# A two-layer attention kernel with new pass timing, one GELU evaluation, scaling on ScalarE, and three PSUM banks for filling units with one for the weighted values

## The chip, the cores and the metric

One core of a Trainium2 chip runs the whole program. The metric is the device time of one execution in microseconds; three executions were timed, and one more was profiled. Engines: TensorE (PE; PEld is its weight loading), VectorE (DVE), ScalarE (ACT), GpSimd (POOL) and SyncE (SP), which only issues DMAs.

## What is computed

Two layers of cross-attention over eight batches of 512 tokens by 512 features, 16 heads of 32. All arithmetic is float32.

```
tgt2 = attention(x Wq', ctx Wk', ctx Wv')[0]       # layer 0: only batch 0 is used
x    = x + tgt2                                    # added to all eight batches
xq, ykv = layer_norm(x, gq, bq), layer_norm(ctx, gkv, bkv)
o    = softmax(q k^T * SCALE) v                    # q = xq Wq, (k, v) = ykv Wkv
x    = x + o Wproj + bproj
h    = gelu(layer_norm(x, gm, bm) W1 + b1)         # exact GELU, 2048 hidden features
x    = x + h W2 + b2
```

## The kernel before

**Precision.** Each float32 operand is split into a high part (rounded to float32r) and a low part (the rest), side by side, and a product is three matmuls (high by high, high by low, low by high). So every evacuation of PSUM is two steps: ScalarE writes the high part, VectorE then subtracts it from the bank and writes the low part. Where a gain and a bias are applied, ScalarE works twice (`affine`), once to the high part and once in place in the bank.

**Passes and ticks.** The attention of layer 0 (batch 0) is pass 0, that of layer 1 for batch n-1 is pass n, 1 to 8. A pass has 16 heads of 4 chunks of 128 keys, 64 ticks. `Plan.core` (L96) puts the three steps of chunk s at three ticks: scores (`ps_s`) at tick t, the transposed, max-shifted weights matmul (`ps_t`) at t + SHIFT, the weighted values (`ps_o`) at t + WEIGH. Between the scores and the weights matmul of a head VectorE takes the row maxima, turns them, and SP sends them by four small DMAs into a row of `q_st` (`load_row`). ScalarE then evaluates the exponential twice, once into the high part `p_hi` and once in place; VectorE makes the low part (POOL for chunk 2 of each head). After the fourth chunk ScalarE moves `ps_o` to `o_raw` (L965, semaphore `o_moved`), and SP's DMAs place it beside the other heads of its group of four (`place_head`); after each group VectorE inverts the sums and POOL joins and scales in four steps (`invert`, `join`).

**Filling units.** All other matmuls are units of 12 matmuls in 4 parts (quarters) of 3, or turns of 4 transposes. Kinds: `a` (turned, normed inputs), `k`, `q`, `v` (projections), `tg` (turned result of pass 0), `out` (projection of the result, Wproj), `ht` (turned, normed h), `hid` (W1), `y2` (W2). `spread` (L81) distributes parts over the three places of each tick: after the scores matmul (0), after the weights matmul (1), after the weighted values (2). Each unit uses one bank of `ps_d`, by its number modulo the number of banks (`bank`, L481), and its first part waits until the unit that had the bank is evacuated. Every pass from 3 on has 16 `hid`, 16 `y2`, 4 `out` and 4 `ht` units of the batch one or two passes back.

**Order.** No engine picks its work: each runs the ticks in order, and within a tick what the tables list, waiting on semaphores. On ScalarE a tick is: evacuations whose unit ended at place 0 or at place 2 of the tick before; a GELU burst; two exponentials; evacuations of units ended at place 1; the `o_raw` move; DMA issues of W1 and W2 pieces (`load_w1`, `load_w2`); the scaling of a norm; weight splits.

**GELU bursts.** Four `hid` units fill one half of `h_st` (128 x 2048). At the burst tick ScalarE evaluates GELU twice over it, into the high part `g_s` (L940) and in place (L941), and POOL subtracts (L1237). Around it ScalarE loads the function table, before the GELU and before the next exponential. The `y2` units placed at the front of the burst tick keep TensorE at work meanwhile. W2 pieces are issued from the tick after the last `y2` unit of the group before, 3 ticks apart.

**Norms.** `norm_ticks` (L249) gives the ticks of statistics (VectorE), inverse deviation (POOL, `inverse_deviation`, L1163) and scaling. The context batches (`y`) and the x batches are scaled by POOL in the staging buffer (`scale_staged`, L1180), the first x batch by VectorE (`scale_x0`), h by ScalarE with `shift` = -mean/deviation as bias (`scale_result`, L918). `X_SUMS` (L324) are POOL's additions of `tgt2` to x.

**The gap.** Between the last weighted values of pass 0 and the first scores of pass 1 are 8 ticks without attention (L128 to L136). There the result of pass 0 is turned (`tg`), added to batch 0 of x, normed, turned (`a10`) and projected (`q1`), stored to DRAM and read back as the first stack (`store`, `load_stack`). A stack is the query and key rows of one head, four DMAs, issued STACK_AHEAD ticks before its scores, once the weights matmuls of the head four before are done. `sync_tables` (L331) gives all ticks of SP's and ScalarE's DMAs.

**Tail.** After pass 8 the last outputs, hidden units and `y2` units run with nothing of a head beside them.

```
                if c == 0:
                    if h >= 2:
                        pe.wait_ge(o_moved, h - 1)
```

These lines (L845 to L847) let TensorE start the weighted values of head h once the head two before has left its bank.

## Time and profile before

| | us |
|---|---|
| median of three timed executions | 2067.64 |
| lowest and highest of them | 2053.57, 2070.22 |
| the profiled execution, its own time | 2060.26 |
| its span, first to last instruction | 2058.3 |

The busy time of an engine is the sum over its instructions, the span is what the metric follows. A matmul's duration overlaps with the next one's, so their pitch is shorter than their mean length. The granted clock is the share of TensorE's full speed that it was given; waits are idle time of an engine with what released it.

### The profile page before, as it was taken

Reading aid. Unit: us, or ns where it says so; the run is one execution under the profiler, and the core shown is the slowest. Engines: PE = TensorE matmul, PEld = TensorE weight load, DVE = VectorE, ACT = ScalarE, POOL = GpSimd, SP = SyncE. Lnnn points to the kernel's source line nnn. Section 1 sums busy time; section 2 is a strip of 40 time slices with the busy share of each in tenths; the row PEclk is TensorE's granted clock in tenths of the full one; section 3 lists DMA queues with packets and bytes.
Section 4 is the critical chain, followed back from the end, with each engine's and each line's share of the span. In section 5 each row is a group of like instructions: output and inputs, shape, how many; then the busy total and the mean of one; then the engine's idle time right before and its main releaser. Section 6 shows DMA issues by size and latency. Waiting matters only on the chain.

```text
span 2058.3 us, 23412 instructions
## 1 busy us (share of the span) xinstructions
PE 1805.1 (88%) x7488; PEld 1365.0 (66%) x7488; DVE 1168.1 (57%) x2008; ACT 1117.8 (54%) x1762; POOL 851.6 (41%) x557
## 2 busy tenths in 40 slices
PE   7899987887887889888899989998988989899898
PEld 5576765665665667666676666676666667677676
DVE  4566654575756556555666565566656656654322
ACT  3455653375656655755665476566556564754211
POOL 0667740477653333434433343433434333433311
PEclk9899998998998899999999999999999999999899
DMA  6689942654643455466366436554663754455243
GB/s 213 227 286 348 381 177 82 204 195 137 209 163 93 141 155 153 134 169 181 114 201 185 146 115 180 165 154 123 195 183 95 205 177 140 137 162 178 94 151 143
DMA packets 156377, 354.65 MB, mean 172 GB/s; under 512 B 28512, under 2 KB 47072, under 8 KB 155360
## 3 DMA queue, kind: packets, MB, share of 16 engines
q1 hardware_dynamic: 119392, 218.92, 34.2%
q10 hardware_dynamic: 36864, 134.23, 20.4%
q8 instruction: 61, 1.00, 0.2%
q14 instruction: 60, 0.49, 0.1%
HBM read 251.51 MB, written 82.08 MB: 162 GB/s over the span
## 4 chain that ended last, share of the span: by engine, by line
PE 57%; DMA 13%; ACT 8%; DVE 7%; POOL 7%; issue 4%; SPq 3%; DVEq 0%; ACTq 0%; POOLq 0%
PE ps_d L806 40%; PE ps_o L855 8%; DMA w_r<-w_scratch 5%; PE ps_t L838 4%; PE ps_s L823 4%; DMA rs<-o_raw 3%; DMA k_st<-k_scratch 3%; POOL stage L1187 2%; SPq L591 1%; DVE p_lo L1117 1%; DVE negmax L1104 1%; ACT ps_t L956 1%; ACT p_hi L950 1%; ACT ps_d L871 1%; POOL stage L1250 1%
## 5 line engine op out<-in xcount | busy, mean ns | idle before, releaser
L950 ACT ACTIVATE p_hi<-ps_t 128x512 fp32r<-128x512 f32 x576 | 344.8, 599 | 571.3 <-PE ps_t L838 569.9
L1225 POOL TENSOR_TENSOR p_lo<-p_full,p_hi 128x512 fp32r<-128x512 f32 x144 | 186.0, 1291 | 717.0 <-ACT p_full L956 714.6
L1104 DVE TENSOR_REDUCE negmax<-ps_s 128x1 fp32r<-128x512 f32 x576 | 388.9, 678 | 130.7 <-PE ps_s L823 129.3
L1117 DVE TENSOR_TENSOR p_lo<-ps_t,p_hi 128x512 fp32r<-128x512 f32 x432 | 297.4, 689 | 267.5 <-ACT ps_t L956 265.9
L806 PE MATMUL ps_d<-hT,w_r 128*128 128x512 f32 x1536 | 438.2, 403 | 12.1 <-DVE hT L991 7.7
L806 PE MATMUL ps_d<-w_r,g_s 128*128 128x512 f32 x1536 | 399.4, 408 | 50.1 <-DMA w_r<-w_scratch 50.0
L806 PEld LDWEIGHTS ps_d<-w_r,g_s 128*128 128x128 f32 x1536 | 302.2, 198 | 128.0 <-DMA w_r<-w_scratch 56.1
L806 PEld LDWEIGHTS ps_d<-hT,w_r 128*128 128x128 f32 x1536 | 297.9, 194 | 91.9 <-DVE hT L991 10.7
L823 PE MATMUL ps_s<-k_st,q_st 96*128 96x512 f32 x576 | 240.2, 417 | 41.2 <-DMA k_st<-k_scratch 36.5
L838 PE MATMUL ps_t<-q_st,k_st 97*128 97x512 f32 x576 | 237.1, 412 | 23.8 <-DVE p_lo L1117 19.0
L956 ACT ACTIVATE ps_t<-ps_t 128x512 f32<-128x512 f32 x432 | 257.9, 597 | 0.0
L855 PE MATMUL ps_o<-p_hi,v_s 128*65 128x512 f32 x576 | 234.6, 407 | 1.1 <-POOL p_lo L1225 1.0
L855 PE MATMUL ps_o<-p_lo,v_s 128*65 128x512 f32 x576 | 231.4, 402 | 0.0
L1237 POOL TENSOR_TENSOR g_s<-h_st,g_s 128x2048 fp32r<-128x2048 f32 x32 | 147.2, 4599 | 114.7 <-ACT h_st L941 114.7
L823 PEld LDWEIGHTS ps_s<-k_st,q_st 96*128 96x128 f32 x576 | 112.0, 194 | 86.8 <-DMA k_st<-k_scratch 45.7
L838 PEld LDWEIGHTS ps_t<-q_st,k_st 97*128 97x128 f32 x576 | 112.2, 195 | 51.0 <-DVE p_lo L1117 22.5
L806 PE MATMUL ps_d<-aT,wq_s 128*128 128x512 f32 x384 | 118.3, 423 | 23.7 <-DVE kq_out L991 22.0
L806 PE MATMUL ps_d<-aT,wk_s 128*128 128x512 f32 x384 | 112.5, 417 | 20.5 <-DVE v_out L991 18.4
L1187 POOL TENSOR_SCALAR stage<-stage,mv,rstd 128x512 f32<-128x512 f32 x60 | 124.2, 2078 | 1.2
L1022 DVE TENSOR_SCALAR h_st<-ps_d,col_s 128x512 f32<-128x512 f32 x128 | 94.5, 738 | 50.8 <-PE ps_d L806 50.8
L806 PE MATMUL ps_d<-wo_s,oT 128*128 128x512 f32 x384 | 110.7, 404 | 14.1 <-POOL oT L1214 12.0
L855 PEld LDWEIGHTS ps_o<-p_lo,v_s 128*65 128x65 f32 x576 | 81.0, 141 | 55.1 <-issue 5.3
(98 smaller groups left out, 2165.5 us busy)
## 6 DMA issues: line engine op xcount, KB each, us to landing
w_r<-w_scratch ACTq DMA_DIRECT2D x256, 512.0 KB, 4.7
v_scratch<-v_out SPq DMA_DIRECT2D x36, 520.0 KB, 4.3
v_s<-v_scratch SPq DMA_DIRECT2D x36, 520.0 KB, 4.5
k_scratch<-kq_out SPq DMA_DIRECT2D x36, 512.0 KB, 4.0
q_scratch<-kq_out SPq DMA_DIRECT2D x36, 512.0 KB, 3.0
q_st<-q_scratch SPq DMA_DIRECT2D x144, 128.0 KB, 2.9
k_st<-k_scratch SPq DMA_DIRECT2D x144, 128.0 KB, 3.2
o_ab<-o_raw SPq DMA_DIRECT2D x144, 128.0 KB, 3.6
```

Source lines behind the costliest of these rows:

```text
L806: ins = nc.tensor.matmul(bank(u), lhs[a], rhs[b], start=(i == 0 and m == 0), stop=(i == 3 and m == 2))
L823: nc.tensor.matmul(ps_s[:, c % 2], q_st[0:KQ, h % G, c * P:c * P + P], k_st[0:KQ, h % G], start=True, stop=True).then_inc(s_ready, 1)
L838: nc.tensor.matmul(ps_t[:, c % 2], k_st[0:KM, h % G, c * P:c * P + P], q_st[0:KM, h % G], start=True, stop=True).then_inc(t_ready, 1)
L855: ins = nc.tensor.matmul(ps_o[0:VW, h % 2], v_s[:, group % 2, c, h % G], src[:, c], start=(c == 0 and m == 0), stop=(c == TC - 1 and m == 1))
L950: act.activation(p_hi[:, c], ps_t[:, c % 2], ACT.Exp, scale=SCALE)
L956: act.activation(whole, ps_t[:, c % 2], ACT.Exp, scale=SCALE).then_inc(p_exp, 1)
L1022: dve.tensor_scalar(h_st[:, done % 2, c % 4], bank(u), col_s[:, 6 * FC + c:6 * FC + c + 1], None, ALU.add).then_inc(evacuated, 1)
L1104: dve.tensor_reduce(negmax[:, h % 2, c:c + 1], ps_s[:, c % 2], AX.X, ALU.max, negate=True).then_inc(s_maxed, 1)
L1117: dve.tensor_tensor(p_lo[:, c], ps_t[:, c % 2], p_hi[:, c].bitcast(F32), ALU.subtract).then_inc(p_split, 1)
L1187: ins = pool.tensor_scalar(buf, buf, mv[:, no % 2, t, 0:1], rstd[:, no % 2, t:t + 1], ALU.subtract, ALU.mult)
L1225: pool.tensor_tensor(p_lo[:, POOL_CHUNK], p_full[:], p_hi[:, POOL_CHUNK].bitcast(F32), ALU.subtract).then_inc(p_pool_split, 1)
L1237: pool.tensor_tensor(g_s[:, done % 2, 1], h_st[:, done % 2], g_s[:, done % 2, 0].bitcast(F32), ALU.subtract).then_inc(g_split, 1)
```

## The change

It re-times the passes and moves work between engines.

- SHIFT 8 to 7, WEIGH 10 to 9, STACK_AHEAD 4 to 5.
- `ps_d` has three banks and `ps_o` one. The first part of a unit waits for the unit three before, and the first weighted values of a head wait for the move of the head before.
- One GELU per burst, in place; the high part is copied from it by four Identity operations of 128 x 512 (`G_HALVES`), one in each of the four ticks behind the burst, and POOL subtracts in the same four pieces. In the tail all four follow at once.
- ScalarE scales all norms (`scaled`), with the bias form; POOL computes `shift` for all of them, and POOL's and VectorE's scaling go.
- The gap has 7 ticks. Its units: `tg` 0 to 2 and eight of the late ones, `tg` 3, then six late ones, `a10` in turn with four late ones, `q1` group 0, then two late ones and two more of `q1`. Seven units that ran in pass 1 are in the gap; two `q` units of batch 8 go between the outs of pass 2.
- Bursts at base + 5, 23, 42, 56 (before 6, 27, 42, 56) with two `y2` units at the front instead of three; outs from tick 14 instead of 16; `ht` units from 24, in turn with `y2` units, instead of from 30.
- W2 pieces 2 ticks apart instead of 3; staging loads, x sums and statistics at other ticks. In the first norm of x VectorE adds `tgt2` as it evacuates each `tg` unit.

```diff
-SHIFT = 8
-WEIGH = 10
+SHIFT = 7
+WEIGH = 9
 POOL_CHUNK = 2
-STACK_AHEAD = 4
+STACK_AHEAD = 5
...
-        spread([gap], [("tg", 0, g) for g in range(G - 1)] + late[:5], front=True)
-        spread([gap + 1], [("tg", 0, G - 1)] + late[5:7], front=True)
-        spread([gap + 2], late[7:9], front=True)
-        spread([gap + 3], late[9:12], front=True)
-        spread([gap + 4], [("a", 10, c) for c in range(FC)], front=True)
-        spread([gap + 5], late[12:13], front=True)
-        spread([gap + 6], [("q", 1, 0)], front=True)
-        spread([gap + 7], late[13:15], front=True)
+        first = [("a", 10, c) for c in range(FC)]
+        for i, units in enumerate(([("tg", 0, g) for g in range(G - 1)] + late[:8], [("tg", 0, G - 1)],
+                                   late[8:11], late[11:14],
+                                   [u for pair in zip(first, late[14:18]) for u in pair], [("q", 1, 0)],
+                                   late[18:] + [("q", 1, 1), ("q", 1, 2)])):
+            spread([gap + i], units, front=True)
...
-        self.base = {n: gap + 8 + (n - 1) * CH for n in range(1, NP + 1)}
+        self.base = {n: gap + 7 + (n - 1) * CH for n in range(1, NP + 1)}
...
-        queries = [("q", 1, g) for g in range(1, G)] + late[15:] + [("a", 11, c) for c in range(FC)]
+        queries = [("q", 1, 3)] + [("a", 11, c) for c in range(FC)]
...
-        spread(range(base[1], base[2] + 16), queries)
+        spread(range(base[1], base[2] + 14), queries[:-2])
...
-                burst(at + 6, old, 2, second(old, 1)[:3])
-                spread(range(at + 7, at + 16), second(old, 1)[3:] + hidden(old, 3)[:3])
-                spread(range(at + 16, at + 26), outs + hidden(old, 3)[3:])
-                burst(at + 27, old, 3, second(old, 2)[:3])
-                spread(range(at + 28, at + 42), second(old, 2)[3:] + turns + hidden(new, 0))
-                burst(at + 42, new, 0, second(old, 3)[:3])
-                spread(range(at + 43, at + 56), second(old, 3)[3:] + hidden(new, 1))
+                burst(at + 5, old, 2, second(old, 1)[:2])
+                spread(range(at + 6, at + 14), second(old, 1)[2:] + hidden(old, 3)[:2])
+                spread(range(at + 14, at + 23), outs + hidden(old, 3)[2:])
+                burst(at + 23, old, 3, second(old, 2)[:2])
+                rest = second(old, 2)[2:]
+                spread(range(at + 24, at + 42), turns[:1] + rest[:1] + turns[1:2] + rest[1:] + turns[2:] + hidden(new, 0))
+                burst(at + 42, new, 0, second(old, 3)[:2])
+                spread(range(at + 43, at + 56), second(old, 3)[2:] + hidden(new, 1))
             else:
-                spread(range(at + 16, at + 26), outs)
-                spread(range(at + 28, at + 42), turns + hidden(new, 0))
+                spread(range(at + 14, at + 23), outs[:1] + queries[-2:-1] + outs[1:3] + queries[-1:] + outs[3:])
+                spread(range(at + 25, at + 42), turns + hidden(new, 0))
                 burst(at + 42, new, 0, [])
                 spread(range(at + 43, at + 56), hidden(new, 1))
-            burst(at + 56, new, 1, second(new, 0)[:3])
-            spread(range(at + 57, at + CH + 6), second(new, 0)[3:] + hidden(new, 2))
+            burst(at + 56, new, 1, second(new, 0)[:2])
+            spread(range(at + 57, at + CH + 5), second(new, 0)[2:] + hidden(new, 2))
...
+G_HALVES = listed([(t + (1 + c if t < PLAN.base[NP] else 0), (n, group, c))
+                   for t in sorted(PLAN.bursts) for n, group in PLAN.bursts[t] for c in range(4)])
...
-    if kind == "y":
-        at = PRE + 1 if i == 0 else PLAN.end("a", 2 + i, 0) - 7
+    if kind == "y" or i and kind == "x":
+        at = PLAN.end("a", (2 if kind == "y" else 10) + i, 0) - 6
+        if i == 0:
+            at = PRE + 1
+        elif (kind, i) == ("x", 1):
+            at = PLAN.gap + 3
...
-X_SUMS = listed([(norm_ticks("x", b)[0][0] - 2 + t // 2, (b, t)) for b in range(1, B) for t in range(TC)])
+X_SUMS = listed([(norm_ticks("x", b)[0][0] - (4 if b > 2 else 3) + t if b > 1 else PLAN.gap + 2, (b, t)) for b in range(1, B) for t in range(TC)])
...
-        stage.append((max(freed, norm_ticks(kind, b)[0][0] - 8), (kind, b)))
+        stage.append((max(freed, norm_ticks(kind, b)[0][0] - (4 if kind == "y" else 9)), (kind, b)))
...
-            second += [(at + (3 * c if at < PLAN.base[NP] else 0), (n, group, c)) for c in range(4)]
+            second += [(at + (2 * c if at < PLAN.base[NP] else 0), (n, group, c)) for c in range(4)]
...
-    ps_o = nc.alloc_psum_tensor("ps_o", [P, 2, T], F32)
-    ps_d = nc.alloc_psum_tensor("ps_d", [P, 2, T], F32)
+    ps_o = nc.alloc_psum_tensor("ps_o", [P, T], F32)
+    ps_d = nc.alloc_psum_tensor("ps_d", [P, 3, T], F32)
 
     def bank(u):
-        return ps_d[:, NO[u] % 2]
+        return ps_d[:, NO[u] % 3]
...
-            if i == 0 and NO[u] >= 2:
-                pe.wait_ge(evacuated, NO[u] - 1)
+            if i == 0 and NO[u] >= 3:
+                pe.wait_ge(evacuated, NO[u] - 2)
...
-                    if h >= 2:
-                        pe.wait_ge(o_moved, h - 1)
+                    if h:
+                        pe.wait_ge(o_moved, h)
...
+        def scaled(kind, i, t):
+            no = NORM_NO[kind, i]
+            if t == 0:
+                act.wait_ge(ln_shift, no + 1)
+                if (kind, i) == ("y", 0):
+                    act.wait_ge(unit_ready, ready("a", 0, FC - 1))
+                elif kind == "h" and i == 1:
+                    act.wait_ge(wo_split, 1)
+                elif kind == "h":
+                    act.wait_ge(unit_ready, ready("ht", i - 1, FC - 1))
+            src, dst = (xres[i % 2], ht) if kind == "h" else (source(kind, i),) * 2
+            ins = act.activation(dst[:, t], src[:, t], ACT.Identity, bias=shift[:, no % 2, t:t + 1],
+                                 scale=rstd[:, no % 2, t:t + 1])
+            if t == TC - 1:
+                ins.then_inc(normed, 1)
...
-                act.activation(g_s[:, done % 2, 0], h_st[:, done % 2], ACT.Gelu)
...
+            for n, group, c in G_HALVES.get(tick, []):
+                done = GELU_NO[n, group]
+                if c == 0:
+                    act.wait_ge(gelu_done, done + 1)
+                act.activation(g_s[:, done % 2, 0, c], h_st[:, done % 2, c], ACT.Identity).then_inc(g_hi, 1)
...
-                act.activation(o_raw[0:VW, h % 2], ps_o[0:VW, h % 2], ACT.Identity).then_inc(o_moved, 1)
+                act.activation(o_raw[0:VW, h % 2], ps_o[0:VW], ACT.Identity).then_inc(o_moved, 1)
...
-                dve.tensor_copy(tgt2[:, :, c * P:c * P + P], bank(u).rearrange("p (t d) -> p t d", t=TC))\
-                    .then_inc(evacuated, 1)
+                added, own = bank(u).rearrange("p (t d) -> p t d", t=TC), slice(c * P, c * P + P)
+                dve.tensor_copy(tgt2[:, :, own], added)
+                dve.tensor_tensor(xt0[:, :, own], xt0[:, :, own], added, ALU.add).then_inc(evacuated, 1)
...
-                    for r in range(TC):
-                        dve.tensor_tensor(xt0[:, r], xt0[:, r], tgt2[:, r], ALU.add).then_inc(x0_summed, 1)
-                    dve.wait_ge(x0_summed, TC)
+                    dve.wait_ge(evacuated, ready("tg", 0, G - 1))
...
-                dve.wait_ge(ln_shift if kind == "h" and i >= 3 else ln_rstd, i - 2 if kind == "h" and i >= 3 else no - 1)
+                dve.wait_ge(ln_shift, no - 1)
...
+            if no >= 2:
+                pool.wait_ge(normed, no - 1)
             if no:
-                pool.wait_ge(ln_rstd, no)
-            if kind == "h" and i >= 3:
-                pool.wait_ge(h_normed, i - 2)
+                pool.wait_ge(ln_shift, no)
             pool.tensor_tensor(var_e[:], mv[:, no % 2, :, 1], eps_s[:], ALU.add).then_inc(ln_eps, 1)
-            if kind == "h":
-                pool.tensor_scalar(m_mean[:], mv[:, no % 2, :, 0], -1.0, None, ALU.mult).then_inc(ln_minus, 1)
+            pool.tensor_scalar(m_mean[:], mv[:, no % 2, :, 0], -1.0, None, ALU.mult).then_inc(ln_minus, 1)
             pool.wait_ge(ln_eps, no + 1)
             pool.tensor_tensor(rstd[:, no % 2], var_e[:], m_half[:], ALU.pow).then_inc(ln_rstd, 1)
-            if kind == "h":
-                pool.wait_ge(ln_minus, i)
-                pool.wait_ge(ln_rstd, no + 1)
-                pool.tensor_tensor(shift[:, no % 2], m_mean[:], rstd[:, no % 2], ALU.mult).then_inc(ln_shift, 1)
-
-        def scale_staged(kind, i, t):
-            no = NORM_NO[kind, i]
-            buf = stage[:, STAGE_NO[kind, i] % 2, t]
-            if t == 0:
-                pool.wait_ge(ln_rstd, no + 1)
-                if (kind, i) == ("y", 0):
-                    pool.wait_ge(unit_ready, ready("a", 0, FC - 1))
-            ins = pool.tensor_scalar(buf, buf, mv[:, no % 2, t, 0:1], rstd[:, no % 2, t:t + 1],
-                                     ALU.subtract, ALU.mult)
-            if t == TC - 1:
-                ins.then_inc(normed, 1)
+            pool.wait_ge(ln_minus, no + 1)
+            pool.wait_ge(ln_rstd, no + 1)
+            pool.tensor_tensor(shift[:, no % 2], m_mean[:], rstd[:, no % 2], ALU.mult).then_inc(ln_shift, 1)
...
-                pool.wait_ge(gelu_done, done + 1)
-                pool.tensor_tensor(g_s[:, done % 2, 1], h_st[:, done % 2], g_s[:, done % 2, 0].bitcast(F32),
-                                   ALU.subtract).then_inc(g_split, 1)
+                pool.wait_ge(g_hi, 4 * done + c + 1)
+                ins = pool.tensor_tensor(g_s[:, done % 2, 1, c], h_st[:, done % 2, c],
+                                         g_s[:, done % 2, 0, c].bitcast(F32), ALU.subtract)
+                if c == 3:
+                    ins.then_inc(g_split, 1)
```

## Rows read from the trace of the kernel before

**Rows 1.** The page's first part, busy time of TensorE, with its share of the span.
```profile
PE 1805.1 (88%) x7488; PEld 1365.0 (66%) x7488; DVE 1168.1 (57%) x2008; ACT 1117.8 (54%) x1762; POOL 851.6 (41%) x557
```

**Rows 2.** Stretches: us, busy time (x instructions) per engine, granted clock, DMA share, GB/s.
```profile
44.50:305.00 260.50, 234.85 (x1017) 177.74 (x1015) 158.96 (x287) 149.24 (x256) 173.22 (x114) 0.97 0.82 284
305.00:372.70 67.70, 47.65 (x194) 36.74 (x193) 26.72 (x46) 19.92 (x31) 3.77 (x4) 0.85 0.30 107
372.70:566.50 193.80, 161.24 (x667) 117.43 (x668) 127.99 (x241) 114.11 (x201) 132.52 (x93) 0.94 0.56 186
...
1301.90:1488.80 186.90, 169.22 (x705) 127.54 (x704) 112.75 (x193) 111.17 (x173) 70.25 (x46) 0.96 0.54 158
...
140.00:260.00 120.00, 110.80 (x491) 84.08 (x491) 80.21 (x140) 70.77 (x125) 89.18 (x57) 1.00 1.02 362
```

**Rows 3.** Who waited for whom, TensorE, 740.1 to 1861.3: us in total, times, longest.
```profile
PE ps_d L806 <- DMA w_r<-w_scratch: 41.8, 17, 6.0
PE ps_s L823 <- DMA k_st<-k_scratch: 25.8, 12, 3.7
PE ps_t L838 <- DVE p_lo L1117: 19.0, 6, 3.5
...
PE ps_d L732 <- DVE hT L991: 7.2, 12, 1.0
PE ps_d L806 <- POOL oT L1214: 5.0, 6, 1.0
```

**Rows 4.** The timeline of TensorE: start, us, line, operation, idle before it.
```profile
1280.81 6.42 PE L806 MATMUL ps_d<-w_r,g_s 128*128 128x512 f32 x27 [1.12 <-DMA w_r<-w_scratch]
...
1321.12 8.70 PE L806 MATMUL ps_d<-w_r,g_s 128*128 128x512 f32 x27 [3.98 <-DMA w_r<-w_scratch]
```

**Rows 5.** The timeline of TensorE, the last steady pass, tick 52.
```profile
1828.35 0.79 PE L823 MATMUL ps_s<-k_st,q_st 96*128 96x512 f32 x1 [2.85 <-DMA k_st<-k_scratch]
```

**Rows 6.** Groups by line and form: count, busy us, mean ns, idle before it and releaser.
```profile
L950 ACT ACTIVATE p_hi<-ps_t 128x512 fp32r<-128x512 f32 x576 | 344.8, 599 | 571.3 <-PE ps_t L838 569.9
...
L940 ACT ACTIVATE g_s<-h_st 128x2048 fp32r<-128x2048 f32 x32 | 61.3, 1914 | 68.7 <-DVE h_st L1022 68.5
...
L940 ACT ACT_TABLE_LOAD x28 | 35.9, 1283 | 0.5
...
L926 ACT ACTIVATE ht<-xres_b,shift,rstd 128x512 f32<-128x512 f32 x16 | 11.7, 804 | 13.0 <-POOL shift L1178 13.0
```

**Rows 7.** The timeline of all engines at the end of a head.
```profile
1002.95 0.58 ACT L965 ACTIVATE o_raw<-ps_o 65x512 f32<-65x512 f32 x1
...
1003.36 0.40 PE L855 MATMUL ps_o<-p_hi,v_s 128*65 128x512 f32 x1
```

**Rows 8.** Who waited for whom, TensorE, whole span.
```profile
PE ps_d L806 <- DVE kq_out L991: 27.5, 22, 3.5
...
PE ps_d L806 <- DVE v_out L991: 18.4, 24, 1.7
```

**Rows 9.** Who waited for whom, TensorE, 300 to 373 us.
```profile
PE ps_d L732 <- POOL o_l L1204: 5.1, 1, 5.1
PE ps_d L732 <- DVE kq_out L991: 4.9, 1, 4.9
...
PE ps_s L823 <- DMA k_st<-k_scratch: 3.3, 1, 3.3
```

**Rows 10.** Who waited for whom, TensorE, pass 1.
```profile
PE ps_d L806 <- DVE kq_out L991: 21.1, 18, 3.5
```

**Rows 11.** Who waited for whom, TensorE, pass 2.
```profile
PE ps_d L732 <- ACT ht L926: 7.2, 1, 7.2
PE ps_s L823 <- DMA k_st<-k_scratch: 6.8, 2, 3.8
PE ps_t L838 <- ACT p_full L956: 4.7, 1, 4.7
PE ps_d L732 <- POOL stage L1187: 3.3, 1, 3.3
```

71 lines of the change are left out of this document (16 added, 55 removed).

## The prediction

> **What bounds the kernel now.** The page's first part comes first: TensorE is busy 88% of the span, and no other engine comes near [rows 1]. What it computes stays the same, so the change can only take waiting away, or add it. The table by stretches shows where the waiting is [rows 2]. The stretches end where the first scores matmul of a pass starts: pass 0 with the first keys and values (44.5 to 305), the gap (to 372.7), passes 1 and 2, one of the six passes 3 to 8 that look alike (184.8 to 189.4 us each; its row stands for all), and the tail from 1861.3. TensorE is idle for 25.7 of 260.5 us in pass 0, 20.0 of 67.7 in the gap, 32.6 of 193.8 in pass 1, 17.7 of 186.9 in a steady pass.
>
> TensorE's waits in the six steady passes (1121.2 us together) name what comes last [rows 3]: W2 pieces 41.8 us, stacks of keys 25.8, VectorE's low halves of the weights 19.0, its evacuation of hT 7.2, POOL's oT 5.0. Per pass: 7.0, 4.3, 3.2, 1.2 and 0.8.
>
> A wait costs more than its length where it is long. Two equal runs of 27 matmuls, 40 us apart, took 6.42 us after a wait of 1.12 and 8.70 after one of 3.98 [rows 4]: 2.3 us more. The granted clock of the pass is 0.96 [rows 2], so part of it ran at the lower level, 1.2 GHz for 2.4. I charge 2 us for each wait of about 3 us or more, an estimate from these two. The undisturbed run gives 0.24 us a matmul, 2.8 us for a unit of 12 and 0.7 for a quarter of one. In these terms a steady pass is 163 us of matmuls (36 units of 2.8, 64 ticks of four matmuls, 2.7 for the turns), about 18 of waits and 6 of slow clock.
>
> **Steady passes, part by part.** Positions are ticks after a pass's base, worked out with the planner's own rule for before and after.
>
> Stacks. STACK_AHEAD 5 with SHIFT 7 issues a head's four loads one tick earlier (2.3 us at 0.94 + two quarters), and now ahead of the previous head's row loads, four DMAs more of lead. There are two waits a pass, one of about 3 us at tick 52 (the last of the six is shown [rows 5]) and one of about 1.2 at tick 4, and both should go: 4.0 us, and the 2 us of slow clock behind the first. Gain 6.0. The row loads themselves lose a tick of lead: wanted five ticks after the last scores matmul before, now four (9 us). TensorE never waited for them before, so I cost this at nothing; its cover is what is left of those 9 us, and if that is gone each us late counts 16 times a pass.
>
> W2. Chunks are issued 2 ticks apart instead of 3. The last one came at tick 5 for the burst at 6, now at 3 for 5: a tick more of lead against a wait of 4.0 to 6.0 us there (six; the shortest stands in [rows 4], the longest is that of [rows 3]), but into transfers as dense as before. I take 5.1 to 2.5. The bursts at 42 and 56 get 6 and 2 ticks of lead instead of 2 and 1, and their 1.9 us (7.0 less 5.1) all but go. Gain 2.6 and 1.7, and 2 of slow clock: 6.3.
>
> Three banks. A unit waits for the evacuation of the third before it. The 1.2 us of turns waiting for hT go [rows 3]. Gain 1.1.
>
> oT. The outs start at tick 14, six ticks after the last weighted values, no longer seven; the chain behind them (move, DMA, join, inverse, three POOL operations) keeps its length. So its wait grows from 0.8 by a tick, less what the denser fill gives back, to 2.8, near where the slow clock begins: loss 2.0 and half of 2.
>
> The burst at 23. Both engines are counted from the weights matmul of tick 21. ScalarE starts when it is out (0.4), does two exponentials (599 ns each, 1.2), waits for POOL's shift (13.0 us in four groups, 3.3) and scales four slices (3.2): 8.1. Then two exponentials (1.2), a table load (1.3), one GELU (1.9), a table load (1.3), two exponentials (1.2), the two evacuations of a turn (1.6, by the scaled form), two exponentials (1.2), a half copy (0.6) and the o_raw move (0.6): 10.9 more, done at 19.0 [rows 6]. TensorE reaches the next head's first weighted values at 14.2 (2.8 for a hidden unit, 5.6 for two y2 units, 3.7 for the sixteen matmuls of the heads, 0.7 for the turn, 1.4 for two quarters). Of the 4.8 between, some 1.7 is a wait for the low half (ready at 15.7), the rest one for the ps_o bank; since ScalarE's operations overlap a little I take 4.4, against 3.2 before: loss 1.2. The GELU taken out (1914 ns) is less than the y2 unit taken from the cover (2.8).
>
> One ps_o bank elsewhere. In the trace of before an o_raw move ends at 1003.53 and the next head's first weighted values start at 1003.36 [rows 7]: one bank would have cost about 0.2 there, and this is the worst ordinary place of a pass; in the others the move ended some 0.5 us or more ahead. A half copy of 0.6 now stands before the move in three more places. Loss 0.8. The Trainium skill (Perfetto Trace Analysis, Matmuls) has a rule that speaks against this part: independent matmul groups should rotate through different banks, so that one's evacuation lies under the next. Taken at its word each head would pay its move, 16 times 0.6 us or 9.6 a pass, and the steady pass would gain nothing; the trace shows the ticks between to be cover enough.
>
> ScalarE as a whole. One GELU of 1914 ns goes and four copies of 0.6 come: 0.5 us more per group, not less; only the burst is shorter, 4.5 us for 6.4.
>
> POOL's low half in four quarters has ten ticks or more until its y2: no cost, that distance is the cover; if it were gone POOL's four operations would stand before the burst.
>
> Net per steady pass: 6.0 + 6.3 + 1.1 - 3.0 - 1.2 - 0.8 = 8.4 us, six times: 50.
>
> **Pass 0.** The waits behind evacuations of values total 18.4 us in 24 pieces [rows 8], nearly all here; three banks remove most. But from 140 to 260 the DMA engines are busy all the time at 362 GB/s [rows 2], and stores of keys and values share them. Between 0 and 16 I take 6: only the part ahead of that stretch. ScalarE gets seven batches of scaling, 3.2 us each, while it is busy 149 of 260.5 us: hidden as long as POOL's shift is there in time.
>
> **The gap.** 5.1 us for the last o_l, 4.9 for a query evacuation, 3.3 for the first stack [rows 9], some 17.6 with the smaller ones (20.0 idle in all), each of the three with 2 of slow clock. Now 8 instead of 5 units stand before the last tg, 6 units (17 us) cover the x0 chain (copy and add, statistics, POOL's inverse, ScalarE's 3.2; before, some 10 us long), and four units (11 us) cover store and load of the first stack. Waits 17.6 to 6, slow clock 6 to 2: gain 15.6. The 7 units more are 19.6 us that pass 1 loses; that cancels.
>
> **Pass 1.** Waits for kq_out are 21.1 us in 18 pieces [rows 10] and go with the third bank. What comes next: per 64 ticks ScalarE has 64 x 1.1 for the pairs of exponentials (the two overlap a little), 16 x 0.6, 22 query evacuations of 0.6, 23 turns of 1.6 and now 24 slices of 0.8: 149 us, TensorE 137. Before: 193.8 - 19.6 = 174 on the same work. So between 149 and 174, I take 162: gain 12.
>
> **Pass 2** [rows 11]. Stacks 6.8 to 0.5 with their slow clock 4: 10.3. The GELU burst without a y2 unit over it 4.7 to 2.8: 1.9. The stage wait 3.3 to 0.5 with its slow clock: 4.8, since ScalarE scales in 3.2 us. ht 7.2 to 6.5, the query evacuations' 27.5 less 21.1 has 3 here. Against it oT 3 and ps_o 0.8. Gain 17.
>
> **Tail.** Its waits are W2 at the same ticks and oT; 2 us for hT.
>
> Sum: 6 + 15.6 + 12 + 17 + 50 + 2 = 103. The profiled execution took 2060.3 (span 2058.3): 1957. The median of the runs is 7 above it, 2067.6: by that 1965. I give 1960, between the two.
>
> **Rivals.** (1) Slower: the one bank. If ScalarE ends each move later than the bank is wanted, every head pays. The margin is about 0.5 us in most heads; from 0.75 us late at all 144 the loss outweighs the 103, and at 0.9 it is 130: 2067.6 - 103 + 130 = 2095. For it: scaling and half copies come before the move in the queue. Against it: ScalarE waits 570 us for TensorE's weights matmuls [rows 6], so it is seldom behind. 7%. (2) ScalarE or VectorE bounds passes 0 to 2, since ScalarE now waits in line for POOL's shift before its exponentials: of the 51 us there some 10 remain: 2000. 19%. (3) Transfers: W2 issued earlier lands no earlier, as the DMA engines are full before each burst; rows for the weights matmul come late now and then. Steady passes then gain 2.5 instead of 8.4: 1995. 13%. (4) The covers all hold (oT 0.8, burst 1.5, pass 1 at 152): 1920. 12%. (5) The orders move and nothing is won, old waits replaced one for one: 2060. 6%. Forecast: 43%.
>
> **Numbers.** 1960, range 1915 to 2030: it leaves out (1), (5) and the ends of the others. A per cent is what a measurement of this kernel can tell. Faster than 2047: 0.87; within 1%: 0.07; slower: 0.06.
>
> **What would show it.** Right: TensorE's wait on k_st near 3 us in all, on w_r in the six passes from 41.8 to under 20, kq_out and v_out under 8 together; a steady pass of 178; granted clock above 0.96; a new wait of ps_o on o_raw of 3 us a pass. Wrong: ps_o waits above 40 us in all; waits of ps_t on row loads; ScalarE idle on POOL's shift in pass 1; oT above 4 a pass.

## The result, and the profile after

| | before | after |
|---|---|---|
| median of the runs, us | 2066.1 (4 runs, 2053.6 to 2070.2) | 1997.0 (4 runs, 1990.8 to 2002.2) |
| ratio | 1 | 0.968 [0.965, 0.972] |
| span of the profiled execution, us | 2058.3 | 1999.4 |
| mean granted clock | 0.949 | 0.949 |

The kernel is 3.2% faster; the forecast said 5.2%. First the profile page's first part and the table by stretches, which answer [rows 1] and [rows 2]. Columns of the second fence: start and end in us, length, busy time (x instructions) of PE, PEld, DVE, ACT and POOL, granted clock, DMA share, GB/s. Its rows are pass 0, the gap, passes 1 and 2, the five passes 3 to 7 together, pass 8 with the tail, one steady pass, and the stretch of full DMA.

```profile
PE 1796.6 (90%) x7488; PEld 1361.1 (68%) x7488; DVE 1165.2 (58%) x2004; ACT 1165.1 (58%) x1922; POOL 749.9 (38%) x625
```

```profile
41.50:290.00 248.50, 229.62 (x1006) 176.53 (x1005) 155.84 (x285) 169.62 (x286) 110.79 (x98) 0.97 0.85 294
290.00:365.20 75.20, 65.17 (x289) 52.74 (x288) 31.64 (x56) 27.39 (x43) 15.74 (x18) 0.93 0.49 173
365.20:519.30 154.10, 137.65 (x592) 99.04 (x591) 120.11 (x227) 127.46 (x223) 72.41 (x71) 0.97 0.60 196
519.30:685.90 166.60, 141.31 (x583) 103.49 (x582) 109.60 (x187) 109.00 (x189) 67.52 (x52) 0.93 0.50 142
685.90:1615.10 929.20, 855.07 (x3522) 643.29 (x3520) 565.95 (x961) 559.20 (x921) 361.46 (x286) 0.95 0.55 159
1615.10:1999.40 384.30, 340.40 (x1400) 264.07 (x1398) 163.78 (x270) 157.85 (x247) 121.71 (x97) 0.93 0.46 148
...
1057.70:1243.30 185.60, 171.08 (x706) 128.97 (x705) 113.12 (x193) 111.84 (x185) 72.29 (x58) 0.94 0.55 160
140.00:260.00 120.00, 111.47 (x484) 84.60 (x484) 77.42 (x143) 78.60 (x137) 63.88 (x51) 0.97 0.99 345
```

The same two long stretches of the kernel before:

```profile
740.10:1676.50 936.40, 846.15 (x3521) 638.77 (x3520) 563.79 (x961) 556.13 (x861) 351.18 (x226) 0.96 0.54 158
1676.50:2058.30 381.80, 339.14 (x1400) 262.64 (x1398) 164.45 (x271) 156.20 (x219) 119.53 (x69) 0.94 0.47 149
```

Set against the forecast, in us gained, with the 19.6 us of work that moved from pass 1 to the gap taken out of both:

| stage | before | after | gained | forecast |
|---|---|---|---|---|
| start | 44.5 | 41.5 | 3.0 | 0 |
| pass 0 and gap | 328.2 | 323.7 (19.6 of it moved in) | 24.1 | 21.6 |
| pass 1 | 193.8 | 154.1 (19.6 moved out) | 20.1 | 12 |
| pass 2 | 173.6 | 166.6 | 7.0 | 17 |
| passes 3 to 7 | 936.4 | 929.2 | 7.2 | 42 |
| pass 8 and tail | 381.8 | 384.3 | -2.5 | 10.4 |
| sum | 2058.3 | 1999.4 | 58.9 | 103 |

The start is scatter: over the kernels run it lay between 40.8 and 44.5 with nothing changed in it. By the counts of matmuls (x) pass 1 kept nine more than the seven units moved out of it account for, and pass 2 has ten fewer, so some 2 us of what pass 2 shows as gained belong to pass 1. The first half came out better than forecast. The passes that look alike, which were to bring half of the gain, brought about a sixth of what was forecast for five of them (7.2 of 42).

TensorE's waits after, whole span (for whom it waited: us in total, times, longest), answer [rows 3] and [rows 8 to 11]:

```profile
PE ps_d L802 <- DMA w_r<-w_scratch: 49.2, 18, 6.5
PE ps_t L834 <- DMA q_st<-negmax_t: 31.4, 19, 3.3
PE ps_d L802 <- POOL oT L1185: 26.2, 7, 7.0
PE ps_t L834 <- DVE p_lo L1102: 20.2, 10, 2.9
PE ps_o L851 <- ACT o_raw L969: 15.4, 17, 1.7
PE ps_d L732 <- ACT ht L925: 7.5, 1, 7.5
...
PE ps_d L802 <- DVE kq_out L994: 1.3, 1, 1.3
```

The waits for an evacuation of `kq_out` or `v_out` are all but gone (`kq_out` 1.3 us here and 4.0 at the turns, `v_out` 0.5), and so are those for the stacks (no row of `k_st` is left). W2 stayed in the first place, at 49.2 us for 54.5. A wait that did not exist before stands second: the row loads (`negmax_t` into `q_st`), 31.4 us.

For passes 3 to 7 the two windows can be balanced. Waits before: W2 35.8, stacks 21.3, `hT` 11.9, low halves 15.9, `oT` 4.1, together 89.0. After: W2 27.2, `oT` 16.1, low halves 12.9, row loads 12.5, `o_raw` 4.5, together 73.2. That is 15.8 less, yet the stretch is only 7.2 shorter: TensorE's own busy time for the same matmuls rose from 846.2 to 855.1, by 8.9, at a granted clock of 0.95 for 0.96. The waits that went were short ones: those above 2 us were 16 before, 60.3 us together, and are 21 now, 64.3 us.

The clock record of the two traces shows where the slow matmuls stand. TensorE was at the lower level, 1.2 GHz, for 71.7 us of the five passes before and for 92.2 after; 20.5 us more at half speed are an estimated 10 us of work, which is the 8.9. By place, summed over the five passes:

| the clock fell at | before, us | after, us |
|---|---|---|
| the first burst (W2) | 30.7 | 27.3 |
| the first out (`oT`) | 0 | 23.9 |
| the second burst (low half, then the `ps_o` bank) | 17.1 | 34.1 |
| the head's stack, tick 51 or 52 | 23.9 | 0 |
| the row load, tick 55 | 0 | 6.8 |

So `oT` took the place of the stacks, and the second burst, where the wait for the low half went from 3.2 to 2.6 us, has slow matmuls for twice as long. The same 15 us around it, pass 5 before and pass 5 after (columns as above, the granted clock third from the end):

```profile
1204.00:1219.00 15.00, 11.05 (x45) 7.59 (x46) 12.00 (x21) 11.84 (x21) 9.90 (x6) 0.89 0.30 83
```

```profile
1140.00:1155.00 15.00, 11.85 (x41) 8.07 (x39) 8.33 (x15) 12.88 (x23) 7.48 (x6) 0.77 0.20 60
```

### The profile page after: what moved, and what is told of

Read it like the earlier page. It is cut to its first block, busy times and chain, and to the rows that moved or that the text cites. A ratio compares the mean times of both kernels' runs of the same rounds, so it can differ in the third digit from the quotient of the medians.

```text
span 1999.4 us, 23652 instructions
## 1 busy us (share of the span) xinstructions
PE 1796.6 (90%) x7488; PEld 1361.1 (68%) x7488; DVE 1165.2 (58%) x2004; ACT 1165.1 (58%) x1922; POOL 749.9 (38%) x625
## 4 chain that ended last, share of the span: by engine, by line
PE 56%; DMA 10%; ACT 9%; issue 8%; SPq 6%; POOL 5%; DVE 5%; ACTq 0%; DVEq 0%; POOLq 0%
PE ps_d L802 39%; PE ps_o L851 8%; DMA w_r<-w_scratch 6%; PE ps_t L834 4%; PE ps_s L819 4%; DMA q_st<-negmax_t 3%; SPq L591 2%; SPq L596 2%; ACT ps_t L955 2%; POOL p_lo L1196 1%; ACT p_hi L949 1%; PE ps_d L732 1%; ACT ps_d L867 1%; DVE negmax L1089 1%; ACT ht L925 1%
## 5 line engine op out<-in xcount | busy, mean ns | idle before, releaser
L802 PE MATMUL ps_d<-w_r,g_s 128*128 128x512 f32 x1536 | 419.4, 412 | 42.7 <-DMA w_r<-w_scratch 42.7
L1196 POOL TENSOR_TENSOR p_lo<-p_full,p_hi 128x512 fp32r<-128x512 f32 x144 | 185.8, 1290 | 698.2 <-ACT p_full L955 698.0
L802 PE MATMUL ps_d<-hT,w_r 128*128 128x512 f32 x1536 | 432.1, 399 | 7.2 <-DMA w_r<-w_scratch 6.5
L802 PEld LDWEIGHTS ps_d<-hT,w_r 128*128 128x128 f32 x1536 | 293.7, 192 | 85.2 <-issue 7.3
L834 PE MATMUL ps_t<-q_st,k_st 97*128 97x512 f32 x576 | 240.6, 418 | 52.0 <-DMA q_st<-negmax_t 31.4
L851 PE MATMUL ps_o<-p_hi,v_s 128*65 128x512 f32 x576 | 237.9, 413 | 18.3 <-ACT o_raw L969 15.4
L819 PE MATMUL ps_s<-k_st,q_st 96*128 96x512 f32 x576 | 235.7, 409 | 3.5 <-DVE negmax L1089 3.1
L1205 POOL TENSOR_TENSOR g_s<-h_st,g_s 128x512 fp32r<-128x512 f32 x128 | 164.5, 1292 | 170.9 <-ACT g_s L962 170.9
L802 PE MATMUL ps_d<-wo_s,oT 128*128 128x512 f32 x384 | 121.8, 437 | 31.5 <-POOL oT L1185 26.2
L851 PEld LDWEIGHTS ps_o<-p_hi,v_s 128*65 128x65 f32 x576 | 80.8, 140 | 59.9 <-ACT o_raw L969 35.6
L802 PEld LDWEIGHTS ps_d<-wo_s,oT 128*128 128x128 f32 x384 | 81.1, 214 | 56.1 <-issue 35.6
```

Source lines behind the costliest of these rows:

```text
L802: ins = nc.tensor.matmul(bank(u), lhs[a], rhs[b], start=(i == 0 and m == 0), stop=(i == 3 and m == 2))
L819: nc.tensor.matmul(ps_s[:, c % 2], q_st[0:KQ, h % G, c * P:c * P + P], k_st[0:KQ, h % G], start=True, stop=True).then_inc(s_ready, 1)
L834: nc.tensor.matmul(ps_t[:, c % 2], k_st[0:KM, h % G, c * P:c * P + P], q_st[0:KM, h % G], start=True, stop=True).then_inc(t_ready, 1)
L851: ins = nc.tensor.matmul(ps_o[0:VW], v_s[:, group % 2, c, h % G], src[:, c], start=(c == 0 and m == 0), stop=(c == TC - 1 and m == 1))
L1196: pool.tensor_tensor(p_lo[:, POOL_CHUNK], p_full[:], p_hi[:, POOL_CHUNK].bitcast(F32), ALU.subtract).then_inc(p_pool_split, 1)
L1205: ins = pool.tensor_tensor(g_s[:, done % 2, 1, c], h_st[:, done % 2, c], g_s[:, done % 2, 0, c].bitcast(F32), ALU.subtract)
```

## The experiments

Two theories stood at the start. A: the bank exchange brings the gain, and the re-timing of the steady passes is eaten by transfers. B: the re-timing brings it, and the single `ps_o` bank costs some of it. Each ratio is against runs of the kernel before on the same chip. The figures by stage come from one profiled execution of each kernel, and those differ among themselves: where the ratios have the whole change 0.5 points (some 11 us) ahead of the banks alone, the two spans are level (1999.4 and 1999.2). So a few us between two kernels in one stage are not a finding.

**The banks alone, and all but the banks.** The first puts the exchange of banks into the kernel before and leaves all else:

```diff
-    ps_o = nc.alloc_psum_tensor("ps_o", [P, 2, T], F32)
-    ps_d = nc.alloc_psum_tensor("ps_d", [P, 2, T], F32)
+    ps_o = nc.alloc_psum_tensor("ps_o", [P, T], F32)
+    ps_d = nc.alloc_psum_tensor("ps_d", [P, 3, T], F32)
```

with `bank`, the wait on `evacuated` and the one on `o_moved` as in the change.

> The kernel before with the bank exchange alone: three banks of ps_d, one of ps_o. Theory: waits of 18.5 us (values) and 22 us (queries) nearly go, 12 us of slow clock in pass 1 with them, hT 1.2 a pass; ps_o costs some 0.3 us a pass: 2066 minus 40 to 55, so 2011 to 2026. In pass 0 between 140 and 260 us the transfers hold part of it back. Rival: without the new order one ps_o bank costs as much as three ps_d banks give: 2055 or more.

Measured: 2000.2 us, 0.974 [0.970, 0.978], which is 2012 by the 2066 that I had started from. TensorE's waits of this kernel:

```profile
PE ps_d L806 <- DMA w_r<-w_scratch: 53.7, 23, 6.8
PE ps_s L823 <- DMA k_st<-k_scratch: 45.0, 24, 3.9
...
PE ps_o L855 <- ACT o_raw L965: 4.0, 11, 0.9
```

The second is the kernel after with the same lines turned back.

> The changed kernel with the banks as before: two of ps_d and two of ps_o, with their waits. Theory: the third ps_d bank is worth the evacuation waits of passes 0 and 1 (18.5 and 20.6 us before) with their slow clock and 1.2 us a pass of hT, less the 15.4 us of ps_o waits: 2025 to 2035 us. Rival: the new order alone took those waits away, and the bank exchange is worth under 10 us: 1997 to 2007.

Measured: 2043.9 us, 0.995 [0.993, 0.998], slower than both theories had it. Its waits:

```profile
PE ps_d L802 <- DVE v_out L994: 26.3, 28, 2.4
...
PE ps_d L802 <- DVE kq_out L994: 25.8, 22, 4.5
PE ps_d L802 <- DVE h_st L1026: 19.3, 6, 3.2
```

So the exchange is worth 2.6% by itself and 2.7 points inside the change (0.995 to 0.968), and everything else is worth about 0.5% with either set of banks. That is theory A; what eats the re-timing comes below. Two things come out that the forecast had not. The exchange also works in steady passes: five of them take 920.3 us with the banks alone, 16.1 less than before, where the whole change takes 929.2. And the denser fill needs three banks: with two a steady pass gets a wait of 3.2 us for `h_st` that neither kernel of the comparison has. The single `ps_o` bank costs next to nothing here: 4.0 us of waits over 144 heads.

By stage (us), banks alone against the whole change: pass 0 and gap 21.6 gained for 24.1, pass 1 10.0 for 20.1, pass 2 5.8 for 7.0, passes 3 to 7 16.1 for 7.2, pass 8 and tail 2.7 for -2.5. The re-timing wins in pass 1, and from pass 3 on it wins nothing and seems to lose; only the difference in pass 1 is well above what single executions differ by.

**The residual's load, seven ticks earlier.** W2's last piece before the first burst came later than its extra tick of lead allows. Here are the piece in pass 5, issued at 1066.37 (the answer for that one load), the matmuls before and after it, and SP's queue:

```profile
L911 ACTq DMA_DIRECT2D w_r<-w_scratch x1: 512/512/512, 1066.4 to 1066.4; - x1
...
DMA to landing us min/median/max: 10.3/10.3/10.3
```

```profile
1036.88 3.70 PE L802 MATMUL ps_d<-w_r,g_s 128*128 128x512 f32 x15 [1.36 <-DMA w_r<-w_scratch]
...
1076.71 5.74 PE L802 MATMUL ps_d<-w_r,g_s 128*128 128x512 f32 x15 [4.51 <-DMA w_r<-w_scratch]
```

```profile
1061.08 0.58 SPq L673 DMA_DIRECT2D xres_a<-x  x1
```

The 1 MB of the residual is issued 5.3 us ahead of the piece, which lands after 10.3 us. In the kernel before, the piece that answers to it (pass 6) was issued at 1316.13, 9.6 us behind the residual, and landed after 4.9. The Trainium skill (DMA: Bandwidth & Descriptors, Queues, rings and completion order) says that each DMA engine takes turns between its queues, a packet at a time; this case agrees as far as it goes: the two loads come from different queues (SP's and ScalarE's), and apart from each other, in the next experiment, both land sooner (the residual of pass 5 in 6.7 us for 10.7). How the engines divide their time no run here shows. The experiment moves only the residual's load, in the kernel after:

```diff
-        res.append((PLAN.base[n + 1], n))
+        res.append((PLAN.base[n + 1] - 7, n))
```

> The changed kernel with the residual load (1 MB of x into xres) issued 7 ticks before the pass instead of at its first tick. Theory: the wait for W2 at tick 5 (4.5 us in pass 5, last piece 10.3 us from issue to landing) is transfers sharing the DMA engines, the residual being 1 MB of what stands before that piece. Then the wait falls to about 1.5 us a pass and its slow clock goes: 4 us for each of six passes, some 1973 us where the changed kernel took 1997. Rival: the last W2 piece lands late by its own distance of two ticks; then the wait stays at 4 us or more and the time within 4 us of 1997. A third way: the residual now meets the row loads at tick 55 and the wait there grows by what the other loses.

Measured: 1956.3 us, 0.952 [0.948, 0.956], 1.6 points better than the change, some 33 us, where I had expected 24. The same piece and its matmuls:

```profile
DMA to landing us min/median/max: 7.6/7.6/7.6
```

```profile
1056.07 5.30 PE L802 MATMUL ps_d<-w_r,g_s 128*128 128x512 f32 x15 [2.29 <-DMA w_r<-w_scratch]
```

```profile
PE ps_t L834 <- DMA q_st<-negmax_t: 25.4, 16, 2.7
PE ps_d L802 <- DMA w_r<-w_scratch: 24.8, 15, 6.5
```

W2's waits fell from 49.2 to 24.8 us, those for rows from 31.4 to 25.4, and the granted clock rose from 0.949 to 0.958. The span fell by 48.3 us, passes 3 to 7 by 30.8: from 185.8 to 179.7 a pass, nearly the 178 of the forecast. The slow matmuls at the first burst all but went, from 27.3 us at the lower clock to 3.4 over the five passes.

The piece's landing of 7.6 us is still not the 4.9 of before. Over the five passes the last piece landed after 9.8 us on average in the change, 6.3 with the residual early and 5.6 in the kernel before, so the residual was the larger part of the delay, not all of it. What else is new beside the piece is a piece of W1. ScalarE's queue before and after (L905 and L901 are W1, L915 and L911 W2, 512 KB each):

```profile
1311.44 0.33 ACTq L905 DMA_DIRECT2D w_r<-w_scratch  x1
1316.13 0.33 ACTq L915 DMA_DIRECT2D w_r<-w_scratch  x1
```

```profile
1066.01 0.33 ACTq L901 DMA_DIRECT2D w_r<-w_scratch  x1
1066.37 0.51 ACTq L911 DMA_DIRECT2D w_r<-w_scratch  x1
```

With two ticks between them, 50 of the 80 W2 pieces of passes 3 to 7 go out right behind a W1 piece; with three it was 20. In the change the 30 others landed after 4.0 to 5.1 us, and 25 with a W1 piece but no 1 MB transfer near after 3.7 to 7.7, median 5.7. The slow ones that are left are those of ticks 50, 53 and 54, with 7.5 to 10.0 us. They follow the store of the pass's output, 1 MB on SP's queue, which went out at tick 46 before and goes out at tick 49 now. The ones that TensorE waited for at the burst of tick 56 are among them: 9.2 to 9.9 us, where before they took 4.3 to 5.0. No run moved the W1 pieces or that store, so their shares are read from the traces and not shown by an experiment.

**The same move beside the banks alone** asks what the rest of the change is worth once the transfers are apart.

> The kernel before with the bank exchange and the residual load issued 7 ticks before the pass; nothing re-timed. The exchange alone gave 0.974, the early load took 1.6% off the changed kernel. Theory: transfers before the burst at tick 6 are the same trouble in the old order, so the load moves the wait of 5 us there too: 0.957 to 0.962, near the 0.952 of the changed kernel with the early load, and the rest of the change is worth under 1%. Rival: the old order gains nothing from it, as its last W2 piece comes only one tick before the burst whatever is in the queues: 0.970 to 0.976.

Measured: 1982.9 us, 0.963 [0.959, 0.968], less than I expected of it. Between this kernel and the change with the same move (0.952) lie 29.7 us of span: 4.2 in pass 0 and the gap, 9.4 in pass 1, 10.5 in pass 2, 1.6 in passes 3 to 7, 5.0 behind them, less 1.1 at the start. So GELU, scaling and new positions bring about 1.1%, most of it in passes 1 and 2 and the tail. In passes 3 to 7 the two are level (900.1 us and 898.4), though not by their waits: TensorE is idle 65.5 us here and 56.0 in the change with the same move, but busy 834.6 against 842.4, since it is at the lower clock for 34.1 us here and 61.4 there. Waits for stacks (22.1 us in these passes) were exchanged for later `oT` and later rows, and what the new waits save in length they lose in slow matmuls.

**The order on SP's queue.** The row loads were costed at nothing, their cover being "what is left of those 9 us". The dearest of them in pass 5: SP's queue, then TensorE.

```profile
1201.88 0.58 SPq L678 DMA_DIRECT2D out<-xres_b  x1
...
1204.70 1.79 SPq L591 DMA_DIRECT2D q_st<-q_scratch  x1
1206.54 0.60 SPq L591 DMA_DIRECT2D k_st<-k_scratch  x1
...
1208.27 2.24 SPq L596 DMA_DIRECT2D q_st<-negmax_t  x4
```

```profile
1217.27 0.52 PE L834 MATMUL ps_t<-q_st,k_st 97*128 97x512 f32 x1 [3.27 <-DMA q_st<-negmax_t]
```

The maxima were turned at 1205.75. The four rows were issued 2.5 us later, behind four loads of the next stack, and TensorE went on only at 1217.27. It is the same head in every pass, the thirteenth of 16: there the rows went out 1.8 to 2.5 us after the turn and TensorE waited 1.4 to 3.3 us, at all others they went out within 0.7 us. At that place the output's 1 MB has just been issued, and an issue itself took long (1.79 us for one that takes 0.6 elsewhere); whether the one comes from the other no run shows. This experiment puts the stacks back behind the rows in the kernel after (`STACK_AHEAD = 5` to `STACK_AHEAD = 4`).

> The changed kernel with STACK_AHEAD back at 4, so that SP issues a head's stack behind the row loads of the head before instead of ahead of them. Theory: the new wait for row loads (31.4 us in all, 19 times) comes half from SP's order (the row at tick 52 was turned at 1205.75 and issued at 1208.27 behind four stack loads) and half from slow landing: it falls to some 10 us, while the stack waits (36.5 us before, gone after) come back by 15 to 25 us; the time stays within 10 us of 1997. Rival: the row wait is the tick that SHIFT took; then it stays above 25 us, the stack waits come on top, and the time is 2015 or more.

Measured: 2026.2 us, 0.985 [0.981, 0.989], 1.7 points worse than the change. Its waits:

```profile
PE ps_s L819 <- DMA k_st<-k_scratch: 29.6, 18, 4.2
...
PE ps_o L851 <- ACT o_raw L969: 25.2, 23, 3.3
```

Waits for rows fell from 31.4 to 6.6 us, those for stacks came back with 29.6, and those for the `ps_o` bank rose by 9.8. The waits moved as my theory had it, the time didn't: I had expected it within 10 us of 1997. The cause of the rows' wait is shown: it is the order on that queue, with the transfers that it puts ahead. The choice of the change is still the better one, since 25 us of waits on rows replace 40 on others.

**The outs one tick later.** On top of the earlier residual, `oT` gets back the tick that the change took:

```diff
-                spread(range(at + 6, at + 14), second(old, 1)[2:] + hidden(old, 3)[:2])
-                spread(range(at + 14, at + 23), outs + hidden(old, 3)[2:])
+                spread(range(at + 6, at + 15), second(old, 1)[2:] + hidden(old, 3)[:2])
+                spread(range(at + 15, at + 23), outs + hidden(old, 3)[2:])
```

> The changed kernel with the early residual load, and in passes 3 to 8 the outs at ticks 15 to 22 instead of 14 to 22. Theory: the oT wait (3.2 us a pass, 0.8 with the old distance) is the tick that the outs lost to the join chain; it falls to 1 us and its slow clock goes: 2 to 4 us for each of six passes against the same kernel with only the early load (ratio 0.952), so 0.943 to 0.948. Rival: the wait only moves into the denser ticks behind it, and the ratio stays at 0.951 or above.

Measured: 1932.5 us, 0.938 [0.935, 0.940], more than expected. The wait in a steady pass, in the change and here, with the same three matmuls behind it:

```profile
1105.24 1.62 PE L802 MATMUL ps_d<-wo_s,oT 128*128 128x512 f32 x3 [3.22 <-POOL oT L1185]
```

```profile
1080.52 0.94 PE L802 MATMUL ps_d<-wo_s,oT 128*128 128x512 f32 x3 [0.95 <-POOL oT L1185]
```

The wait fell from 3.2 to 0.95 us, and passes 3 to 7 from 179.7 to 176.7 us, 3.0 each: 2.3 of this wait, 0.7 of its three matmuls alone (1.62 to 0.94) and 0.5 at the low half, while the rows wait 0.8 longer. The clock no longer falls at the first out (23.9 us at the lower level over the five passes before this edit, none after it), and over the whole kernel it is now 0.965.

**VectorE's inversion in the gap.** The gap's longest wait kept its place and its 5.1 us [rows 9], though five units became eight before it. All engines there, in the kernel after:

```profile
315.79 0.69 DVE L994 TENSOR_TENSOR v_out<-ps_d,v_out 128x512 fp32r<-128x512 f32 x1 [2.06 <-ACT v_out L862]
316.40 0.70 DVE L1061 STREAM_TRANSPOSE rs_t<-rs 128x512 f32<-128x512 f32 x1
...
318.74 1.26 POOL L1175 TENSOR_TENSOR o_l<-o_ab,rs 128x512 f32<-128x512 f32 x1 [20.46 <-POOLq L1176]
320.15 1.09 PE L732 MATMUL ps_d<-id_s,o_l 128*128 128x128 f32 x4 [5.11 <-POOL o_l L1175]
```

POOL had joined the sums by 298.3 and stood idle 20.5 us. VectorE took them up at 316.40, right behind the evacuation of the last unit of the same tick, since its program issues all of a tick's evacuations first. More units ahead of the wait only pushed the inversion back with them. The experiment (with the earlier residual) lets VectorE invert behind the fifth evacuation of that tick:

```diff
-            for u in EVACUATED.get((tick, False), []):
+            for i, u in enumerate(EVACUATED.get((tick, False), [])):
+                if tick == PLAN.gap and i == 5:
+                    for n, g, step in INVERTS.get(tick, []):
+                        invert(n, g, step)
                 evacuate(*u)
...
-            for n, g, step in INVERTS.get(tick, []):
+            for n, g, step in INVERTS.get(tick, []) if tick != PLAN.gap else []:
                 invert(n, g, step)
```

> The changed kernel with the early residual load, and VectorE inverting the sums of the last group of pass 0 behind five of the gap tick's twelve evacuations instead of behind all of them. Theory: the last tg waits 5.1 us in both kernels although three units more stand before it, because the inversion is queued behind the evacuations of those very units (it ran at 316.4, right behind the last one at 315.8, while POOL's join was done at 298.3). Then this wait goes to zero and the kernel gains 5 to 7 us on the one with the early load alone. Rival: the chain of DMA and join is what takes the time; then the wait stays at 3 us or more.

Measured: 1952.2 us, 0.947 [0.944, 0.951]. The inversion starts at 300.03, the wait for `o_l` is gone, and pass 0 with the gap is 4.5 us shorter. The whole is not measurably better than without it (0.952, intervals overlap): the cause of the gap's wait is shown, its worth in the total is within the scatter of the rest.

**GELU once or twice.** In the kernel after, the second GELU comes back and the four copies go:

```diff
+                act.activation(g_s[:, done % 2, 0], h_st[:, done % 2], ACT.Gelu)
                 act.activation(h_st[:, done % 2], h_st[:, done % 2], ACT.Gelu).then_inc(gelu_done, 1)
...
-                act.activation(g_s[:, done % 2, 0, c], h_st[:, done % 2, c], ACT.Identity).then_inc(g_hi, 1)
```

> The changed kernel with GELU evaluated twice in the burst, the high part directly, and no Identity copies. Theory: the copies are worth what the shorter burst gives: with 1.9 us more in the burst and only two y2 units over it the waits at the four bursts grow by about 1.9 us each where they exist (ticks 23 and 42 above all), the ps_o waits shrink by 1: 20 to 30 us slower than the changed kernel, ratio 0.978 to 0.983 against 0.968. Rival: ScalarE is never the bound, one GELU or two is the same; ratio 0.966 to 0.972.

Measured: 2001.4 us, 0.970 [0.967, 0.974], the same as the change, where I had expected a loss of over a per cent. Its waits:

```profile
PE ps_t L834 <- DVE p_lo L1098: 32.3, 10, 4.7
...
PE ps_o L851 <- ACT o_raw L965: 9.1, 13, 1.7
```

The wait for the low half at the second burst grew from 2.6 to 4.4 us a pass (all such waits: 32.3 for 20.2), and the waits for the `ps_o` bank fell from 15.4 to 9.1, as no copies stand before the move. W2's waits were 42.7 for 49.2. The single GELU shortens that wait by 1.8 us; that the copies give most of it back, through the `ps_o` bank, fits these figures and is not shown apart.

**Scaling on POOL.** In the kernel after, the staged slices are scaled by POOL again, the shift and all positions as in the change:

```diff
+                if kind == "h" or (kind, i) == ("x", 0):
+                    scaled(kind, i, t)
```

> The changed kernel with the scaling of the staged context and x batches back on POOL (mean and deviation form), at the ticks of the change. Theory: in passes 0 and 1 ScalarE's scaling gives POOL 124 us back; with norms only 6 ticks ahead of their turns POOL's 8.3 us a batch comes late, each late batch costs 2 to 4 us: 10 to 30 us slower, ratio 0.973 to 0.983. Rival: it was hidden either way and pass 1 even gets faster, as the ps_o waits there (6.3 us) shrink: ratio 0.964 to 0.969.

Measured: 2025.1 us, 0.983 [0.980, 0.986]. Its longest waits:

```profile
PE ps_d L732 <- POOL stage L1171: 45.1, 12, 8.3
```

Pass 1 takes 170.2 us for 154.1, pass 0 and the gap 329.5 for 323.7, pass 2 173.5 for 166.6. In the kernel before, POOL's scaling was waited for 7.3 us in all, so most of these 45.1 belong to the new positions: once the turns come sooner, POOL no longer scales in time, and ScalarE does. The two edits carry each other, and neither can be priced alone.

**Together.** The earlier residual, the later outs, the earlier inversion, and in pass 2 the outs at ticks 16 to 24, the turns from 27 and the queries to 16:

> The early residual load, the outs a tick later, the early inversion, and in pass 2 the outs at ticks 16 to 24 and the turns from 27 (14 to 22 and 25 before; TensorE waited 5.3 us for oT there and 7.5 for ht). Theory: the parts add, as they lie in different places: 0.938 of the early load with later outs, less 0.002 for the inversion and 0.002 for pass 2: 0.933 to 0.936. Rival: pass 2's wait for ht is its own chain behind the outs and only moves with them, and the inversion's gain drowns: 0.937 to 0.939.

Measured: 1919.5 us (six runs, 1913.5 to 1927.7), 0.932 [0.928, 0.936]. Pass 2 fell from 164.3 to 158.4 us against the version with the earlier residual alone, pass 0 and the gap from 322.2 to 317.0, passes 3 to 7 to 176.3. This is the fastest kernel of the study, 3.7% below the change by the two ratios.

## Why the prediction came out as it did

**Direction and range held, the size did not.** 1997 lies in the range of 1915 to 2030, 37 us above the forecast, next to rival (3), W2 landing no earlier and rows coming late, at 1995; and it is that rival's mechanism that two experiments showed. That its number fits so well is in part luck: passes 3 to 8 and the tail brought 48 us less than forecast, more than this rival took off, pass 2 another 10 less, and pass 1 8 more. Of the marks named for the forecast, `k_st` (none left) and `kq_out` with `v_out` (5.8 for "under 8") were met; a steady pass of 178 (185.8), W2 under 20 (34.0 in the six passes), a clock above 0.96 (0.949) and a `ps_o` wait of 3 us a pass (0.9) were not; and "waits of ps_t on row loads", named as a sign against it, appeared.

**W2, 6.3 a pass, failed at its first step**: "a tick more of lead [...] I take 5.1 to 2.5". It measured 4.5 in pass 5 and 4.2 on average, for 5.2 before. All of the W2 waits in passes 3 to 7 went from 35.8 to 27.2, 1.7 a pass for the 4.3 that I had counted as waits. Of the later bursts, the one at 42 lost its wait; the one at 56 kept it, 5.7 us over the five passes for 5.9, though its pieces were issued sooner. What failed is "into transfers as dense as before". The residual's 1 MB, which the same edit had brought from 9.6 to 5.3 us ahead of the last piece, spent the tick of lead at the first burst: with it away W2's waits in the five passes are 12.3 and the pass is 179.7. The pieces for the burst at 56 have a W1 piece right ahead and the output's 1 MB, now three ticks later, before that. I had counted ticks of lead for each load and not listed what else is in flight.

**Row loads, "I cost this at nothing", failed**: 31.4 us in all, 12.5 in passes 3 to 7, in six waits of up to 3.3, at one head a pass and not at sixteen. The text named the cover (9 us) and what its loss would cost, but did not measure the chain: 2.5 us behind the stack loads on SP, then the landing, 11.5 from turn to matmul. The gain on stacks (4.0 of waits a pass) was right to 0.3 and came at this price.

**oT, 0.8 to 2.8, was near**: 3.2, but the slow clock that I had charged at half of 2 us was there in every pass, 4.8 us at the lower level on average (estimated cost 2.4), and the experiment took it away with the wait.

**The burst, 3.2 to 4.4, was too dear in waits and too cheap in all**: 2.6 for the low half and 0.5 to 1.4 for the bank are 3.1 to 4.0, but the clock behind it stayed low for 6.8 us a pass instead of 3.4. That is an estimated 1.7 us more, which the sum had at nothing, and no experiment took it away: it is still 6.1 a pass with the outs later. **The bank elsewhere** was forecast at 0.8 a pass; 15.4 us of `o_raw` in all is what burst and bank together bring, and none of the marks of rival (1) was met (over 40 us). The rule of the Trainium skill named in the prediction (Perfetto Trace Analysis, Matmuls) is half borne out: it holds for `ps_d`, where a third bank brought 2.6%, and the move from `ps_o` is so well covered that its single bank cost 4.0 us of waits in the old order and 15.4 in the new one.

**Pass 1, 12, was under-sized**: 20.1. "149 us" for ScalarE was the step: it was busy 127.5 of 154.1 us, TensorE 137.7 (I had 137). ScalarE's groups in pass 1 of the kernel after (count, busy us, mean ns, idle before it), of which the first shows 56 pairs of exponentials where I had counted 64:

```profile
L949 ACT ACTIVATE p_hi<-ps_t 128x512 fp32r<-128x512 f32 x56 | 33.5, 598 | 13.7 <-PE ps_t L834 12.5 <-PE ps_o L851 1.0
...
L925 ACT ACTIVATE stage<-stage,shift,rstd 128x512 f32<-128x512 f32 x28 | 21.1, 809 | 3.8 <-POOL shift L1161 3.7
```

That is 8.8 us too many. And the groups of this window together are 145.8 us while the engine's busy time is 127.5: its operations overlap by 18.3 in all, and I had let them do so only inside a pair. With a bound so far off, rival (2) had too high a chance as well: ScalarE waited 3.7 us for POOL's shift there. Of the 20.1 the banks alone bring 10.0, the new orders the rest.

**Pass 0 and the gap, 21.6, came to 24.1** with two errors that cancel: pass 0 gave 12.0 for the 6 forecast, the gap 12.1 for 15.6. Idle time fell in pass 0 from 25.7 to 18.9 and in the gap from 20.0 to 10.0. The `o_l` wait of 5.1, which eight units instead of five were to cover, stayed whole, for the reason shown above.

**Pass 2, 17, came to 7.0.** The stacks' 6.8 went, but rows took 4.0, the outs waited 5.3 for `oT` where I had put 3 (the profile names no releaser; the `oT` that they read was finished 0.1 us before they went on), `ht` stayed at 7.5, the low halves cost 3.9 and the `ps_o` bank 3.3. Its outs and turns moved two ticks later gave 5.9 us.

**The tail, 10.4 with pass 8, came to -2.5**: W2's waits there are 22.1 for 18.7, `oT` 10.2 for 7.9.

**Slow matmuls** were charged at 2 us for each wait "of about 3 us or more", by [rows 4]. The price held at W2: fifteen matmuls took 5.74 us after 4.51 of wait and 3.70 after 1.36. The bound of 3 us did not: after a wait of only 2.29 they took 5.30, 1.6 more, and at the second burst the clock fell in all five passes after 2.6. Nor did the length of the wait tell the price there, 3.4 us at the lower clock after 3.1 to 3.5 of wait before and 6.8 after 2.6 now. This is why 15.8 us less of waits gave 7.2 of time in passes 3 to 7. What decides between the two no run shows.

**The GELU swap**, counted as 1.9 us off the burst less the work taken from its cover, is worth 0.2% [-0.3, 0.7] by the two ratios, which can't be told from nothing.

Open: how much of W2's landing the W1 pieces and the output's store cost, and why the clock stays low for longer behind the second burst than before; and the `ht` wait of 7.5 in pass 2, which stayed at 7.1 to 7.5 in every run.

## What to carry to other kernels

Before counting on a tick more of lead for a load, list every transfer that will be in flight with it, the large ones that run once a pass first, and every issue ahead of it on the same queue: an earlier issue is worth little when it lands beside a megabyte, as here, where a tick more of lead took 1 us off a wait of 5.2. In an in-order engine, more work in front of a wait covers it only if the work that ends the wait isn't queued behind that same work. And price a wait with the slow matmuls behind it, and read the granted clock around each wait that a change brings or moves: here one wait of 4.5 us cost 2 us more than its length, and one of 1.4 nothing more.

## What the runs showed of the hardware

A 512 KB piece of W2 landed in 10.3 us with a 1 MB load issued 5.3 us ahead of it on another queue, and in 7.6 with that load 22.6 us ahead, both with a W1 piece of 512 KB issued 0.36 us ahead on its own queue; in the kernel before, with the 1 MB 9.6 us and the W1 piece 4.7 us ahead, it landed in 4.9. Fifteen float32 matmuls of 128x512 took 3.70, 5.30 and 5.74 us after waits of 1.36, 2.29 and 4.51: TensorE runs at 2.4 GHz in the first and partly at 1.2 GHz in the others, so the fall comes at a wait shorter than I had taken. The mean granted clock over a whole kernel was 0.949 in the change, 0.958 with the residual early and 0.965 with the outs later as well, as TensorE spent 205, 164 and 137 us at the lower level. It does not simply follow the length of the waits: in passes 3 to 7 the banks alone with the residual early have 42.4 us of waits above 2 us and 34.1 us at the lower level, the change with the residual early 33.9 and 61.4.
